# GpSimd's affine passes over four graphs, issued as one instruction per graph

## The reference, cut to what matters

```
h = relu(layernorm(x));  x = x + elu(attention0(h, adj))         # the branch, once per graph
h = relu(layernorm(x))
for l in 0, 1, 2:                                                # three layers
    scores = leaky_relu(si[:, None] + sj[None, :] + b);  attn = softmax(masked scores)
    u = x + attn @ x
    h = (u - mean) * rstd * g1[l] + beta1[l]                     # affine pass 1
    v = h + gelu(h @ W1[l] + b1[l]) @ W2[l] + b2[l]
    x = (v - mean) * rstd * g2[l] + beta2[l]                     # affine pass 2
out = x_before + x                                               # residual, after the last layer
```

## Time and profile before

| | |
|---|---|
| three timed executions | 3079.88, 3086.2, 3086.65 us; median 3086.2 |
| span of the profiled execution, first to last instruction | 3084.0 us (no device time of this execution is given beside it) |
| DVE busy | 2835.6 us, 92% of the span |
| PE busy | 2773.8 us, 90% |
| POOL busy | 1653.8 us, 54% |
| mean granted TensorE clock | 0.959 of full speed |

### The profile page before, as it was taken

The page is one execution under the profiler, slowest core; times in us unless marked ns, Lnnn a source line. Parts: engine busy times, 40 slices in busy tenths (PEclk is TensorE's granted clock), DMA queues, the critical chain, the costliest instruction groups (busy, mean ns, idle before and its releaser), DMA issues.

```text
span 3084.0 us, 52575 instructions
## 1 busy us (share of the span) xinstructions
PE 2773.8 (90%) x16868; PEld 2449.8 (79%) x16868; DVE 2835.6 (92%) x8596; ACT 1947.7 (63%) x3594; POOL 1653.8 (54%) x998
## 2 busy tenths in 40 slices
PE   4598999999999999999899999999989999989898
PEld 3387888887878888888787888888778888888887
DVE  5999999999999999999999999999999988888996
ACT  4686666666666667666666666666666655555553
POOL 2354555565565565555565455556566545453545
PEclk9799999999999999999999999999999999999999
DMA  6422111222121212112222121212222111111111
GB/s 190 154 83 67 59 62 66 72 64 83 57 86 58 71 57 66 54 59 72 90 72 71 48 67 57 71 59 78 69 71 73 59 37 41 43 35 46 46 59 48
DMA packets 120313, 209.70 MB, mean 68 GB/s; under 512 B 12992, under 2 KB 85728, under 8 KB 120032
## 3 DMA queue, kind: packets, MB, share of 16 engines
q1 hardware_dynamic: 120032, 206.26, 20.8%
HBM read 118.15 MB, written 88.08 MB: 67 GB/s over the span
## 4 chain that ended last, share of the span: by engine, by line
DVE 53%; PE 30%; issue 9%; ACT 5%; DMA 1%; DVEq 0%; POOL 0%; SPq 0%; POOLq 0%; ACTq 0%
PE bank L581 16%; PE bank L566 9%; DVE e L814 9%; DVE g_lo L855 8%; DVE st L832 7%; DVE ub L844 4%; DVE ub L920 4%; DVE ub L827 4%; DVE xo L844 3%; DVE cc L806 3%; DVE mv L837 2%; DVE zt_lo L956 2%; PE ps_u L541 1%; DVE vb L904 1%; DVE nm L892 1%
## 5 line engine op out<-in xcount | busy, mean ns | idle before, releaser
L581 PE MATMUL bank<-w_hi,g_hi 128*128 128x256 f32 x3072 | 901.6, 293 | 6.2 <-DVE g_lo L855 4.7
L581 PE MATMUL bank<-w_hi,g_lo 128*128 128x256 f32 x3072 | 876.3, 285 | 0.0
L581 PE MATMUL bank<-w_lo,g_hi 128*128 128x256 f32 x3072 | 875.9, 285 | 0.0
L1043 POOL TENSOR_TENSOR rs<-ve,neg_half 128x4 f32<-128x4 f32 x256 | 267.0, 1043 | 1124.9 <-DVE ve L840 1120.0
L687 ACT ACTIVATE g_hi<-bank,b_eff 128x512 fp32r<-128x512 f32 x768 | 528.5, 688 | 490.2 <-PE bank L566 469.9
L566 PE MATMUL bank<-zt_hi,w_hi 128*128 128x512 f32 x1536 | 664.8, 433 | 128.3 <-DVE vb L904 88.8
L566 PE MATMUL bank<-zt_hi,w_lo 128*128 128x512 f32 x1536 | 623.2, 406 | 0.0
L566 PE MATMUL bank<-zt_lo,w_hi 128*128 128x512 f32 x1536 | 622.9, 406 | 0.0
L581 PEld LDWEIGHTS bank<-w_hi,g_hi 128*128 128x128 f32 x3072 | 591.8, 193 | 13.6 <-DVE g_lo L855 12.8
L581 PEld LDWEIGHTS bank<-w_lo,g_hi 128*128 128x128 f32 x3072 | 591.9, 193 | 0.7
L581 PEld LDWEIGHTS bank<-w_hi,g_lo 128*128 128x128 f32 x3072 | 590.8, 192 | 0.0
(11 more groups left out here) (96 smaller groups left out, 4925.0 us busy)
## 6 DMA issues: line engine op xcount, KB each, us to landing
xb<-x_scratch SPq DMA_DIRECT2D x96, 512.0 KB, 4.1
x_scratch<-xo SPq DMA_DIRECT2D x69, 512.0 KB, 4.9
xin<-in_x SPq DMA_DIRECT2D x40, 512.0 KB, 4.5
r_scratch<-elu_r SPq DMA_DIRECT2D x32, 512.0 KB, 3.0
xin<-r_scratch SPq DMA_DIRECT2D x32, 512.0 KB, 5.8
out<-xo SPq DMA_DIRECT2D x32, 512.0 KB, 5.1
m<-m_scratch SPq DMA_DIRECT2D x96, 128.0 KB, 2.0
x_scratch<-h SPq DMA_DIRECT2D x24, 512.0 KB, 2.6
```

Source lines behind the costliest of these rows:

```text
L581: mm = pe.matmul(y, g[:, c, r * P:(r + 1) * P], w[:, l, c, :], start=(c == 0 and n == 0), stop=(c == C - 1 and n == 2))
L1043: pool.tensor_tensor(rs[:, :], ve[:, :], neg_half[:, :], ALU.pow).then_inc(rs_ready, 1)
```

## The change

Each pass of GpSimd over a unit was one instruction over 128 x 1024 elements, the row of 256 values broadcast over the four graphs. Now a helper, `by_graph`, issues four instructions of 128 x 256 elements, one per graph; only the last of the four tells the semaphore. The waits stand where they stood, ahead of the first of the four. This holds for all five kinds of pass: the scale and shift of `xo` (two per unit), the residual (one per unit of the last layer), and the scale and shift of `hb` (two per unit). In the last unit the same helper is used on VectorE.

```diff
-        def all_graphs(row):
-            return row.unsqueeze(1).to_broadcast((P, T, D))
+        def by_graph(eng, dst, src, other, op):
+
+            for t in range(T):
+                ins = eng.tensor_tensor(dst[:, t, :], src[:, t, :], other(t), op)
+            return ins
...
             eng.wait_ge(z2_ready, st.nth(u))
-            eng.tensor_tensor(xo[:, :, :], xo[:, :, :], all_graphs(g2_row[:, l, :]), ALU.mult).then_inc(xo_scaled, 1)
+            by_graph(eng, xo, xo, lambda t: g2_row[:, l, :], ALU.mult).then_inc(xo_scaled, 1)
             eng.wait_ge(xo_scaled, st.nth(u))
-            eng.tensor_tensor(xo[:, :, :], xo[:, :, :], all_graphs(beta2_row[:, l, :]),
-                              ALU.add).then_inc(xo_shifted if last else xo_ready, 1)
+            by_graph(eng, xo, xo, lambda t: beta2_row[:, l, :], ALU.add).then_inc(xo_shifted if last else xo_ready, 1)
             if last:
...
-                eng.tensor_tensor(xo[:, :, :], xo[:, :, :], xin[1][:, :, :], ALU.add).then_inc(xo_ready, 1)
+                by_graph(eng, xo, xo, lambda t: xin[1][:, t, :], ALU.add).then_inc(xo_ready, 1)
...
-                    pool.tensor_tensor(h[:, :, :], ub[:, :, :], all_graphs(g1_row[:, l, :]), ALU.mult).then_inc(h_scaled, 1)
+                    by_graph(pool, h, ub, lambda t: g1_row[:, l, :], ALU.mult).then_inc(h_scaled, 1)
...
-                    pool.tensor_tensor(h[:, :, :], h[:, :, :], all_graphs(bb_row[:, l, :]), ALU.add).then_inc(h_ready, 1)
+                    by_graph(pool, h, h, lambda t: bb_row[:, l, :], ALU.add).then_inc(h_ready, 1)
```

## The result

The changed kernel takes 2939.07 us (median of four runs, 2936.16 to 2941.41) against 3086.3 before: a ratio of 0.9523, 95% interval 0.9507 to 0.9538. That is 147 us less, where 92 were forecast.

A forecast was written before the change was run, and what follows sets the result against it. DVE, 92% busy, was taken to be held by POOL's affine passes, about 360 us. Terms 49 + 47 + 7 + 2 - 13 = 92 us took the span from 3084 to 2992, so 2994 us; range 2940 to 3080.

The forecast's parts named there:

- The mechanism: DVE instructions wait, counted busy, for a whole two-input POOL pass; split, they wait for one piece; forecast's chance 0.68.
- closed ranks: Rival: nothing gets in between POOL pieces without a gap, so held instructions wait 2.9 us, not 2.4; 3195 us, chance 0.13.
- the absorbed change: Rival: queued pieces' heads are hidden and keep the port, a pass of four stays 2.4 us; 3086 us, chance 0.05.
- it gets in: A waiting DVE instruction is served between two POOL instructions without a gap, read from line 799 beside line 1043.
- The price of a piece: A two-input POOL instruction over 256 elements takes 0.75 us, between 0.61 and 1.31; half a microsecond more per pass.
- Middle steps: 24 steps where xo's pieces meet four e instructions: done 2.05 us earlier each, 49 us gained.
- Uniform steps: 20 steps at the end: about 27.5 us instead of 30.6, 47 us gained in 15, 7 in five.
- The five with the residual's pass: Uniform steps where four more pieces fall on dots: 1.5 us gained each, 7 us together.
- Early steps: 24 steps where all eight pieces fall on a row of 17 instructions: 4.3 us held against 4.4, nothing gained.
- Late steps: 24 steps: 2 us gained at the second normalisation; in the last layer line 1043 comes later, 13 us lost.
- its own lower bound of 2952: Case of 0.61 us a piece: each hold 0.14 shorter, 42 us more gained in uniform and middle steps.

## Why the prediction was right, and where it was not

**The mechanism** stood as forecast: whole passes hold DVE instructions to their end, a waiting one gets in between pieces without a gap, one per piece. The rival of closed ranks (3195 us) and the absorbed change are out by the timeline above. But the row that tipped the forecast toward "it gets in" could not carry it. Line 799 was served although line 1043 had just started; yet line 1043 does not hold such instructions, since line 801 runs beside it in 0.16 us. The right rival was chosen on evidence that could not tell the two apart, and in that the forecast had luck. The Trainium skill's sentence that each of GpSimd's cores starts its next instruction when its own share is done (GPSIMD Engine Reference, "Instruction dispatch") does not keep DVE out here: the four pieces of 2.96 us let three or four DVE instructions through.

**The price of a piece**: 0.75 taken, 0.74 measured for hb's scale and 0.80 for xo's pieces; 0.5 us more per pass, 0.55 measured.

**Middle steps**: 49 us forecast, 49 measured alone. The exact match is partly luck, since the steps themselves are 2.30 us shorter instead of 2.05 and others give a little back.

**Uniform steps, the step that failed first**: 54 forecast, 74 measured alone. The term's held time afterwards was set too high. The working had 8.1 us held per step; the trace has 1.06 (808) + 0.17 (842) + 1.6 (normalisation) + 1.6 (e) + 2.4 (dots) = 6.8. Each hold by a piece was set at 0.6 to 0.75 for e, where it is 0.53 throughout, and line 840's hold was kept at 0.5. DVE's free work was right (19.6 us), and so was that both idle times go: 19.5 + 6.8 = 26.3. Against the forecast's 27.5 that is 1.2 us too much in the 15 plain steps (47 us forecast, 64 by their step lengths). The five with the residual's pass were marked down to 1.5 us each, where they gained 2.2. PE's row is full in the plain steps too (341.4 of 341.4 us), so 26.3 us is where both engines meet.

**Early steps, the second**: nothing forecast, 26.5 us measured alone. The working counted only held time on DVE (4.3 against 4.4, right within 0.3) and not who waits for the instruction nm between the dots. Its earlier end frees ACT, and DVE's own wait for ACT goes. What the term left out is DVE's waiting for ACT, 14.2 + 96.0 us before and 2.2 + 79.5 with this split alone. That both waits shrink is read from the traces; no run shortens the hold of nm alone.

**Late steps**: 13 us of loss in the last layer did not come. The rows that this term was read from the earlier trace rows are not of a late step: they are the start of step 47, an early step, as the input's statistics and line 892 further on in it show. The third pass follows a late step's second normalisation and runs at the start of the next step. So the loss had to show in the early steps with three passes (20, 23, 44, 47, 68 and 71). They went from a mean of 36.7 to 36.4 us, while the other early steps gained 0.6: about 0.3 us lost in each of six, instead of 1.6 in eight. The timeline of POOL in step 20 of the changed kernel, answering to the earlier trace rows, and of DVE, to the earlier trace rows:

```profile
743.39 2.81 POOL L357 TENSOR_TENSOR xo<-xo,xin 128x256 f32<-128x256 f32 x4
746.16 1.02 POOL L1045 TENSOR_TENSOR rs<-ve,neg_half 128x4 f32<-128x4 f32 x1
```

```profile
743.21 0.17 DVE L842 TENSOR_SCALAR ve<-mv 128x4 f32<-128x4 f32 x1
...
745.57 0.66 DVE L808 TENSOR_TENSOR cc<-small 128x4 f32<-128x4 f32 x1
...
747.22 1.38 DVE L846 TENSOR_SCALAR ub<-ub,mv,rs 128x256 f32<-128x256 f32 x1 [0.32 <-POOL rs L1045]
```

Line 1045 does start 2.8 us behind its input, but the one who needs it, the first normalisation, waits only 0.32 us, since DVE has other work until then. The working charged the whole delay of line 1043 to the step and not the part that outlasts DVE's other work. With eight pieces per pass these six steps do have such waits, 3.3 to 3.7 us each.

**The range** reached down to 2940 and its own lower bound of 2952 came from a piece of 0.61 us. The miss was not in that price. Of its 55 us, 20 are in the uniform steps and 26.5 in the early ones; the rest, about 8, is the late steps' term: 2 - 13, a loss of 11, was forecast, and about 3 are left when the three measured terms are taken from the total. The bounds had nothing for a wait of another engine that goes away.

## What to carry to other kernels

When tiny VectorE instructions show means of a microsecond, hold their ends against those of GpSimd's instructions: if they coincide, the length of that GpSimd instruction is a price that VectorE pays. Look at each kind of GpSimd instruction by itself, since here the inverse roots and the mask passes held nobody to their end. Split the GpSimd work that meets a short run of such instructions, or whose victim others wait for; leave whole what meets a run as long as the number of pieces, or whose result is urgent. Then count not only the time held but who waits for each held instruction: here DVE's own idle time was 83 us of the 150 that the span lost.

## What was not expected of the hardware

A one-input GpSimd pass over 128x1024 fp32 takes 1.1 us, a two-input one 2.4, and both hold VectorE to their end. The mask passes over 128x512, also with one tensor input, take 1.94 and 2.02 us and do not; neither does line 1043, 1.0 us over four elements. Once DVE's holds are short, the uniform step stops at 26.2 us in four different kernels (xo in eighths, with the low halves in two pieces too, one-input passes, and all passes in eighths), and this step no longer answers to what is taken off DVE: PE has no idle time in it, at a clock of 1.00.
